# Keeping two convolution tiles token phase by token phase, so that their turns to token order load neighbouring words

## The reference

```python
x = x + _L0_conv_ref(_ln_c(x), weight, gamma, beta, mean, var)
#   _ln_c: normalise over the 64 channels of each pixel
#   conv:  n -> BN(conv3x3(sign(n), scale * sign(weight))) + n
t = x.reshape(32, 64, 3136).transpose(0, 2, 1)        # tokens: one per pixel
t = t + _L0_ffn_ref(_ln_t(t), ...)                    # long causal filters along the tokens, by FFT
out = t.transpose(0, 2, 1).reshape(x.shape)
```

## Time and profile before

| | |
|---|---|
| median of 3 runs | 1821.32 us (1821.08 to 1821.56) |
| the profiled execution's own time | 1804.83 us |
| its span | 1802.9 us |
| PE busy | 1447.2 us (80%) |
| DVE busy | 1293.6 us (72%) |
| ACT busy | 992.4 us (55%) |
| POOL busy | 546.8 us (30%) |

### The profile page before, as it was taken

The page is one execution under the profiler, slowest core; times in us unless marked ns, Lnnn a source line. Parts: engine busy times, 40 slices in busy tenths (PEclk is TensorE's granted clock), DMA queues, the critical chain, the costliest instruction groups (busy, mean ns, idle before and its releaser), DMA issues. The chain is left out here.

```text
span 1802.9 us, 42890 instructions
## 1 busy us (share of the span) xinstructions
PE 1447.2 (80%) x16769; PEld 1074.4 (60%) x16769; DVE 1293.6 (72%) x1818; ACT 992.4 (55%) x1781; POOL 546.8 (30%) x475
## 2 busy tenths in 40 slices
PE   2668888888888886839899999999999994754667
PEld 1344444444444443228788888888888883754667
DVE  4598888888888889697688888888888881322223
ACT  1446666566656664565577766677776661211222
POOL 1258778778777876000000000000000000000000
PEclk9889999999999998569999999999999996877788
DMA  8115655665555554604533333443333326889986
GB/s 153 17 72 136 147 143 130 134 133 121 118 118 118 135 138 101 130 1 154 172 103 103 103 105 111 113 122 113 103 103 103 103 78 168 239 294 297 290 266 236
DMA packets 169852, 248.80 MB, mean 138 GB/s; under 512 B 10181, under 2 KB 149799, under 8 KB 158311
## 3 DMA queue, kind: packets, MB, share of 16 engines
q1 hardware_dynamic: 158294, 189.04, 41.0%
q0 software_dynamic: 11520, 59.25, 10.4%
HBM read 129.20 MB, written 119.06 MB: 138 GB/s over the span
## 5 line engine op out<-in xcount | busy, mean ns | idle before, releaser
L930 POOL DMA_DIRECT2D w_scratch<-wf x64 | 38.7, 610 | 716.9 <-DVE wf L1135 716.9
L1116 ACT ACTIVATE hf<-ring 64x512 f32<-64x512 f32 (+1 forms) x384 | 228.0, 594 | 48.9 <-PE ring L990 42.0
L1295 DVE TENSOR_TENSOR out_sb<-p_out,out_sb 128x392 f32<-128x392 f32 x128 | 72.5, 567 | 223.7 <-PE p_out L1271 223.7
L990 PEld LDWEIGHTS ring<-v_mov,m_sta 99*128 99x128 f16 x6144 | 196.7, 98 | 22.2 <-issue 19.3
L546 PE MATMUL p_conv<-signs_padded,conv_w 128*128 128x448 bf16 x1008 | 198.2, 354 | 11.7 <-ACT conv_y L612 11.7
L990 PE MATMUL ring<-v_mov,m_sta 99*128 99x64 f16 x6144 | 200.5, 193 | 3.0 <-DVE hf L1135 1.5
L650 POOL TENSOR_TENSOR conv_y<-conv_y,x_in 128x448 f32<-128x448 f32 x112 | 180.6, 1627 | 39.9 <-ACT conv_y L612 32.6
L1284 ACT ACTIVATE out_sb<-p_x 128x392 f32<-128x392 f32 x128 | 63.7, 497 | 232.5 <-PE p_x L1262 226.2
L1135 DVE COPY hf<-ring 128x512 f32<-128x512 f32 (+1 forms) x256 | 175.0, 684 | 5.8 <-PE ring L990 0.9
L518 PE MATMUL p_rt<-ident,conv_y 128*98 128x128 f32 x512 | 91.7, 319 | 101.0 <-DVE x_t L731 53.9
L1271 PE MATMUL p_out<-last_masked,w_in 128*128 128x98 f32 x1024 | 149.9, 294 | 26.7 <-DMA w_in<-w_scratch 26.7
(11 more groups left out here) (148 smaller groups left out, 2950.6 us busy)
## 6 DMA issues: line engine op xcount, KB each, us to landing
z_in<-z_scratch SPq DMA_DIRECT2D x32, 1041.5 KB, 6.7
z_scratch<-z_sb SPq DMA_DIRECT2D x16, 2048.0 KB, 15.3
w_scratch<-wf POOLq DMA_DIRECT2D x64, 512.0 KB, 6.3
w_in<-w_scratch SPq DMA_DIRECT2D x16, 2048.0 KB, 19.0
x_in<-in_x SPq DMA_DIRECT2D x16, 1568.0 KB, 11.0
x_scratch<-x_t SPq DMA_DIRECT2D x16, 1568.0 KB
out_dram<-out_sb POOLq DMA_DIRECT2D x16, 1568.0 KB, 12.1
x_in<-x_scratch SPq DMA_DIRECT2D x12, 1568.0 KB
```

The source lines that it names most:

```text
L990: mm = nc.tensor.matmul(bank[:, NF * i:NF * i + NF], m_sta[m][:, 8 * k + i, :], v_mov[v][:], start=(n == 0), stop=(n == 2))
L1116: return nc.scalar.activation(dst, src, ACT.Copy, scale=scale)
L1295: nc.vector.tensor_tensor(to, view(p_out[:, c % BANKS, :]), to, ALU.add).then_inc(summed, 1)
```

## The change

The tiles x_cen and conv_y get the shape 32 phases x 98 tokens. Word (a, b) of a partition is token 32 b + a, where before the word's place was the token's number. A chunk of the convolution, 448 tokens, is then 14 values of b for each of the 32 phases: 32 runs of 14 words, 98 words apart. Whoever writes a chunk reads its source at a step of 32 words: ACT from PSUM, POOL from x_in. The turns read 98 neighbouring words per phase where they read every 32nd. Counts of instructions, waits, transfers and sizes stay as they are.

```diff
-        x_cen = sb("x_cen", [128, TOK])
-        conv_y = sb("conv_y", [128, TOK])
+        x_cen = sb("x_cen", [128, NA, NB])
+        conv_y = sb("conv_y", [128, NA, NB])
...
+        CB = CW // NA
+
+        def phase_major(tile, c):
+
+            return tile[:, :, CB * c:CB * c + CB]
+
+        def by_phase(v):
+
+            return v.rearrange("p (b a) -> p a b", a=NA)
+
...
-                    mm = nc.tensor.transpose(p_rt[0:NB, c % 2, 128 * j:128 * j + 128], conv_y[:, a:TOK:NA],
+                    mm = nc.tensor.transpose(p_rt[0:NB, c % 2, 128 * j:128 * j + 128], conv_y[:, a, :],
                                              keep["ident"][:])
...
-                        mm = nc.tensor.transpose(p_xt[0:NB, c % 2, 128 * j:128 * j + 128], x_cen[:, a:TOK:NA],
+                        mm = nc.tensor.transpose(p_xt[0:NB, c % 2, 128 * j:128 * j + 128], x_cen[:, a, :],
                                                  keep["ident"][:])
...
-                    nc.scalar.activation(x_cen[:, CW * c:CW * c + CW], p_cen[:, c % 2, 0:CW],
+                    nc.scalar.activation(phase_major(x_cen, c), by_phase(p_cen[:, c % 2, 0:CW]),
                                          ACT.Copy).then_inc(cen_saved, 1)
...
-                    nc.scalar.activation(conv_y[:, CW * c:CW * c + CW], p_conv[:, c % 2, 0:CW], ACT.Identity,
+                    nc.scalar.activation(phase_major(conv_y, c), by_phase(p_conv[:, c % 2, 0:CW]), ACT.Identity,
                                          bias=keep["bn"][:, 1:2], scale=keep["bn"][:, 0:1]).then_inc(y_saved, 1)
...
-                    v = conv_y[:, CW * c:CW * c + CW]
-                    nc.gpsimd.tensor_tensor(v, v, x_in[slot][:, CW * c:CW * c + CW], ALU.add).then_inc(r_done, 1)
+                    v = phase_major(conv_y, c)
+                    nc.gpsimd.tensor_tensor(v, v, by_phase(x_in[slot][:, CW * c:CW * c + CW]), ALU.add).then_inc(r_done, 1)
```

## The result

The changed kernel takes 1864.3 us (median of 4 runs, 1857.5 to 1878.8) where the kernel before takes 1821.4 (4 runs). The ratio is 1.024, 95% interval 1.016 to 1.031: slower, by something between 1.6 and 3.1%. Its profiled execution took 1857.5 us against 1804.8, 52.7 us more.

A forecast was written before the change was run, and what follows sets the result against it. The prediction took a per-pair loop through DVE, its chain set by the length of POOL's adds, as the bound. It summed 51 + 2.6 + 2.1 to 56 us over 1821.3, giving 1877 us, range 1820 to 1920.

The forecast's parts named there:

- Nothing from the turns: Weight loads of the turns (L534, L518): contiguous words bring no gain, as loads overlap matmuls at a 0.11 us pace.
- Nothing from ACT: ACT's copies (L588, L612): reading PSUM at 128 bytes and writing runs of 14 costs nothing.
- POOL's add, 1.13 to 1.50 us: POOL's add of x_in into conv_y (L650): the 32-word step lengthens it from 1.13 to 1.50 us.
- What the longer add does to a pair: DVE's chain up to L722: longer adds leave shorter gaps and hold more short instructions, 3.65 us more per pair.
- the walk with 1.50 us: Step-by-step timing of one pair's POOL adds and DVE instructions: L722 ends at 330.97 instead of 327.31 us.
- two SBUF inputs: DVE beside POOL's adds: an instruction reading two SBUF operands that meets an add ends just behind it.
- Everything moves rigidly, since PE idles there already: Behind L722 in a pair: L691, L731, ACT's copies and the next convolution shift unchanged; 14 x 3.65 = 51 us.
- carrying that difference over unchanged: Whole time: the profiled execution's 16.5 us under the median was kept, so the loss was added to 1821.3 us.
- the add with a doubled second stream: Rival at L650: add 1.31 us, L722 2.75 us late, 41 us more, 1862 us; within the 0.58 for 1.25 to 1.75.
- Saturation: Rival at L650: adds above 1.72 us never pause, DVE gets one instruction per add; 1929 us at 2.0 us; chance 0.14.
- That POOL does not mind: Rival at L650: the strided read costs nothing, the add stays at 1.13 us, total 1821 us; chance 0.16.
- the change is faster: Rival at the turns: POOL unaffected and contiguous weight loads shorten turns, 1808 to 1816 us; chance 0.06.

The follow-up runs named there:

- e1: Changed kernel with only x_cen phase by phase, conv_y and POOL's add as before: 1816.4 us, ratio 1.0016 to the kernel before.
- f4: Changed kernel, but ACT leaves token order in a three-chunk ring and POOL reorders on its write to conv_y: 1814.8 us, ratio 0.998 to the kernel before.
- e3: Changed kernel, but POOL's add reads x_in as neighbouring words, so the residual goes to wrong tokens: 1806.7 us, ratio 0.997 to the kernel before.
- e4: Kernel before, with each of a pair's seven POOL adds given its own word order (x_in steps 1 to 32; one strides conv_y): 1852.0 us, run once.
- h1: Kernel before, with DVE's reciprocal root for x_cen kept in PSUM, so these instructions have at most one SBUF operand: 1758.6 us, ratio 0.970.
- h2: Changed kernel, with DVE's reciprocal root for x_cen kept in PSUM: 1772.9 us, ratio 0.979 to the kernel before.
- e2: Changed kernel with only conv_y phase by phase, x_cen as before: 1869.3 us, ratio 1.031 to the kernel before.
- g2: Kernel before (token order) without POOL's adds; PE adds x_in in the turns by identity matmuls: 1958.5 us, ratio 1.079.
- g1: Changed kernel without POOL's adds; PE adds x_in in the turns by identity matmuls: 1900.9 us, ratio 1.046 to the kernel before.

## Why the prediction was right

*Nothing from the turns.* Right as far as can be told. The loads got shorter, 162 to 127 ns, and e1 and f4 show no gain beyond their intervals, which leave room for 1 us (e1) and 7 us (f4).

*Nothing from ACT.* Right: 7 ns a copy, and e1 and e3 stay level.

*POOL's add, 1.13 to 1.50 us.* The mechanism was right and the size was off: 1.38 us, 0.25 more where I took 0.37, and inside the range of 1.13 to 1.87 that the rows gave. Taking the middle between no effect and a word's whole work was a choice without a row behind it. The estimate from the Trainium skill ("GPSIMD Engine Reference", performance pitfalls) gave the same 1.50 us and is too high by as much. Its threshold, steps over 8 bytes, agrees with e4 (1.14 us at 8 bytes, 1.35 at 16; no step between was tried).

*What the longer add does to a pair.* Right in kind: one short instruction in a gap where two were, the first three adds back to back, and L722 behind the last add. From the end of L713 to that of L722 a pair took 13.5 us before (313.81 to 327.31) and takes 16.4 now (331.73 to 348.12), 2.9 us more, where the walk with 1.50 us had 3.65. The Trainium skill ("SBUF — State Buffer", who interferes with whom) says that a DVE instruction with two SBUF inputs contends with a POOL instruction that reads SBUF; h1, where the nine Newton steps and the two L722 have one input in PSUM and none is held, agrees. The prediction took two SBUF inputs for what all held instructions share, and they do not: L151, L152 and L717 read a single one and are held as well (1.35, 1.29 and, in h2, 6.79 us). In h1 L151 still reads SBUF but writes to PSUM, and is not held. The reductions L713 and L691, from SBUF to SBUF, are never held: 2.27 to 2.29 us in all pairs.

*"Everything moves rigidly, since PE idles there already."* This was the step that failed. Before the third turn chunk PE stands idle for 8.1 us (346.4 to 354.5) where it stood 2.7 (331.0 to 333.7), and its granted clock is at the lower level, 1.2 GHz, from 348.6 to 358.8 us, where it was from 333.4 to 336.8 (columns as in the stretch above):

```profile
348.60:358.80 10.20, 4.29 (x12) 2.80 (x13) 7.46 (x10) 0.98 (x2) 4.14 (x13) 0.50 0.00 0
```

Most of that is idle time, but 4.3 us of work fall into it instead of 3. Behind the wait the first two matmuls of `center` take 1.70 us in both kernels, the next two 1.45 us where they took 0.92. From the end of L722 to the end of the last L731 a pair takes 14.3 us instead of 13.7, and DVE's wait for the turns rose from 52.2 to 62.1 us in all, 0.6 a pair. So 2.9 + 0.6 = 3.5 us, against a measured 3.4: the predicted 3.65 came that close by two errors of opposite sign, an add taken too long and a cost of the turns left out. That was luck.

*The sum.* The fourteen pairs lost 49.8 us (I had 51) and the first two 3.5 (I had 4.7), 53.3 in all against the forecast 56. In the profiled executions the difference is 52.7. The medians differ by 43, since the execution profiled before was 16.6 us under its median and the one after 6.8 under; carrying that difference over unchanged cost the forecast ten of its 13 us of error.

*Rivals.* The nearest was the add with a doubled second stream, 1.31 us. The measured 1.38 lies nearer to it than to 1.50, and the measured 2.9 us up to the end of L722 nearer to its 2.75 than to 3.65. Its 1862 us is nearer to the median of 1864.3 than the forecast is, but only through the carried difference: its sum of 41 us misses the 52.7 of the profiled executions by more than the 56 do. Saturation, put at an add of 1.72 us and more, was not reached. That POOL does not mind is refuted by e2 against e3, that the change is faster by e1 and f4.

## What to carry to other kernels

Before changing the order of words for the sake of one reader, list every engine that reads or writes the tile and its partners: here the reader that gained had slack, and the one that paid held up the busiest engine. Look for DVE instructions that take several times their usual length beside POOL's work: their cure is an operand in PSUM or a shorter POOL instruction (3% here from the operand, 3.5% from halving the add, which leaves out half the work), and a reordering that must be done on POOL belongs on its write. A stall that grows on one engine can cost again on TensorE, through its clock.

## What the runs showed that I had not expected

- An f32 matmul with the identity loads its weights twice. Strided by 32 words each such pass takes 0.17 us, contiguous 0.11, and g2 (both operands strided) takes 57.6 us more than g1 (one strided); the transposition, one pass, goes at 0.11 us either way. The same layout is worth nothing in the one and 3% in the other.
- A held DVE instruction can sit through several of POOL's: 6.79 us for an f32 tensor_scalar from SBUF to SBUF, against 0.23 us for an int32 one that writes to PSUM. How many it sits through varies, and what decides it no run shows. L151, L152 and L164 of the changed kernel each end just behind one add, though the first three adds follow each other at once (332.39 to 336.49 us above), while L717 in h2 waited for a pause.
- POOL's strided write, 448 words at a step of 98, takes 1.142 us against 1.132 for neighbours.
